# Another order at the entry of the tree-expert stage, node-logit bias on ScalarE, five sums of x on GpSimd

## The chip, the cores and the metric

The kernel runs on one core of one Trainium2 chip. The metric is the device time of one execution in microseconds (us), and less is better. The core's engines are TensorE (PE, with its weight loads as PEld), VectorE (DVE), ScalarE (ACT), GpSimd (POOL) and SyncE (SP). Each has a queue of its own and works it off in order; they wait for each other by semaphores only.

## The reference, cut to what matters

The program is a stack of four layers on 1250 tokens of width 512: a graph network with batch norm, routed experts, a second graph aggregation, and a tree of experts. Only the last one is touched by the change. In short:

```python
def _leaf_probs(flat_x, rw, rb):                 # 7 nodes, 8 leaves
    for d in range(3):
        logits = flat_x @ rw[off:off+n].T + rb[off:off+n]
        p = sigmoid(logits)
        leaf = (leaf[:, :, None] * stack([1 - p, p], 2)).reshape(n_tok, 2 * n)
x  = x + aggregate(layernorm(x)) @ weight.T      # the layer before, "produce" in the kernel
f  = layernorm(x)
h  = gelu(einsum('nd,edh->neh', f, w1) + b1)     # 8 experts, 512 -> 2048
y  = einsum('neh,ehd->ned', h, w2) + b2          # 2048 -> 512
x  = x + einsum('ned,ne->nd', y, leaf)
```

## The kernel before, in words

The tree stage is `phase_tree` (from L1603). Its work is cut by hidden columns: 64 groups G of 256 columns, eight for each expert. For each G, TensorE computes the first layer and for each pair of groups (a quarter Q) the second. Every float32 product is split into a high and a low part, and `cut_products` (L526 to L530) makes three matmuls of it.

The first layer is a fast matrix product. The tokens lie in three blocks of 418, 418 and 414 and x (transposed, `f_xT`) in four slices of 128. From these VectorE makes 20 sums, the forms (`x_forms`, by `total` L2222 and `less_both` L2226), with eight helper sums (`x_parts`). ScalarE rounds the forms in ten pairs to a high part (`form_highs`, L1830) and VectorE takes the low part (`form_lows`, L2231). Each pair is 836 columns wide. The forms are needed in the order of `FORM_ORDER`: pair 0 is forms 6 and 11, then 18 and 15, and so on. 15 sums of the weights are made for each G by GpSimd (`weight_sums`, L1772), rounded by ScalarE (`w_high`, L1838), and VectorE takes the rest in three instructions (`w_rest`, L2104): two on raw weights, one on the 14 sums, 1792 columns wide. `first_layer(G)` on TensorE waits at its start for all three of its G (`w_lo >= 3 * (G + 1)`).

TensorE then multiplies 20 forms in an order written by hand. Product names follow the PSUM bank that they close: D B1 C1 A1 (forms 6, 11, 18, 15), A2 (5), E (10), B2 (9), A3 (13, 16), B3 (0, 4), A4 (7), F (14), B4 (17), A5 (1, 19), B5 (2, 8), C2 (3), A6 (12). Between products VectorE adds banks into `hidden` in the order T12 T00 O00 T02 O02 T01 T11 V O12 O01 O11 (the `mix_` functions), and ScalarE copies banks out (P6, V, P18, F2, F6, A4). Product A2 waits for T12, B3 for F6, A4 for T00, B5 for T01.

Before that comes the entry of the stage. For each of the ten token tiles TensorE runs `produce` (the layer before), VectorE adds it to `x_rows` and takes the statistics, ScalarE writes normalized rows, TensorE turns them (`turn`, L1972), and ScalarE copies them into `f_xT` (`moved`, L1864). `logits(b)` (L1982) multiplies the node weights with token block b, `node_logits(b)` (L2219) adds the bias from `rb_col`, and `node_turn(b)` (L1989) turns the result. ScalarE makes the branch probabilities from it (L1922), and GpSimd the leaf weights (L1818, L1822).

All orders are written out by hand, one list for each engine, in one block with no scheduler. On SP the next raw weights are loaded once VectorE is through with the old: `load2(1)` waits for `w2_rest(0)`, and `load1(2)`, behind it, for the two raw parts of `w_rest(1)` and the sums of GpSimd.

Of the kernel before, what the change touches and what calls it, by code (L numbers as in the profile page):

```python
# [1602 lines left out]
def phase_tree(nc, sem, g, produce, rows):  # L1603
# [49 lines left out]

    FORM_ORDER = (6, 11, 18, 15, 5, 10, 9, 13, 16, 0, 4, 7, 14, 17, 1, 19, 2, 8, 3, 12)
    FORM_AT = {form: i for i, form in enumerate(FORM_ORDER)}
    SUMS = counts("A B F8 E F16 F F1 F5 H I F6 C F11 F7 F18 G F15 F10 F3 F14 F9 F13 F17 F4 F19 F2 F12")
    PART_AT = {name: 2 + i for i, name in enumerate("HICGEFAB")}

    U1, U2, U3, U4, U5, U6, U7, U8, U9, U10, U11, U12, U13, U15, H0K0, H1K0, H0K2, H0K3 = range(WFORMS)
# [75 lines left out]
    with nc.Block() as block:  # L1735
        @block.sync
        def _(sp):
            def load1(n):
                e, p = divmod(n, 8)
                if n:  # L1740
                    sp.wait_ge(w_lo, 3 * (n - 1) + 2)
                    sp.wait_ge(w_sum, w_summed(n - 1, "U13"))
                sp.dma_start(raw1[:, :, :], w1_d[e, :, :, p * 256:(p + 1) * 256]).then_inc(w1_in, 16)

            def load2(n):
                e, p = divmod(n, 8)
                if n:
                    sp.wait_ge(w2_lo, n)
                sp.dma_start(raw2[:, :, :], w2_d[e, :, 2 * p:2 * p + 2, :]).then_inc(w2_in, 16)

            load1(0)
            load2(0)
            load1(1)
            for G in range(GROUPS):
                if G % 8 == 0:
                    e = G // 8
                    if e == 0:
                        sp.wait_ge(node_turned, 1)
# [12 lines left out]

        @block.gpsimd  # L1772
        def _(q):
# [53 lines left out]

        @block.scalar
        def _(a):
            def form_highs(p, *after):  # L1830

                for name in after:
                    a.wait_ge(x_sum, SUMS[name])
                a.activation(form_high(2 * p, 2 * p + 2), g.xsum[:, 2 * p:2 * p + 2, :], ACT.Copy).then_inc(x_hi, 1)  # L1834

            def w_high(n):
# [10 lines left out]
            def w2_high(n):  # L1847
                a.wait_ge(w2_in, 16 * (n + 1))
                if n == 0:
                    a.wait_ge(x_sum, len(SUMS))  # L1850
                    a.wait_ge(noded, 3)
                if n >= 2:
                    a.wait_ge(used, y_count(n // 2 - 1, NT - 1))
                a.activation(w2hi[:, n % 2], raw2[:, :, :], ACT.Copy).then_inc(w2_hi, 1)

            for i in range(NT + 3):
                j = i - 2
                if 0 <= j < NT:
# [12 lines left out]
                if i == 7:
                    a.wait_ge(moved, 4)
                    a.activation(form_sum(0), x_block(2, 2), ACT.Copy, scale=-1.0).then_inc(x_unit, 1)
            a.wait_ge(produced, NT)
            form_highs(0, "F6", "F11")
            form_highs(1, "F18", "F15")
            form_highs(2, "F5", "F10")
            form_highs(3, "F9", "F13")
            a.wait_ge(x_unit, 1)
            form_highs(4, "F16")  # L1880
            form_highs(5, "F4", "F7")
            form_highs(6, "F6", "F14", "F17")
            form_highs(7, "F11", "F15", "F1", "F19")
            form_highs(8, "F16", "F19", "F2", "F8")
            form_highs(9, "F17", "F3", "F12")

            def bias(G, j):
                at = G // 8 * 16 + G % 8 * 2 + j
# [77 lines left out]
        def _(t):  # L1966
# [115 lines left out]
            t.wait_ge(added, 8)  # L2082
            logits(1)
            turn(8)
            t.wait_ge(added, NT)
            node_turn(0)
            turn(9)
            logits(2)
            node_turn(1)
            node_turn(2).then_inc(node_turned, 1)  # L2090
            t.wait_ge(moved, NT)
            for G in range(GROUPS):
# [9 lines left out]

        @block.vector
        def _(v):  # L2104
            def w_rest(n):
                to, of = g.wlo[n % 2], g.whi[n % 2]
                v.wait_ge(w_hi, 3 * n + 1)
                v.tensor_tensor(to[:, H0K0:H1K0 + 1, :].rearrange("p u c -> p (u c)"), raw1[:, 0, :],
                                of[:, H0K0:H1K0 + 1, :].rearrange("p u c -> p (u c)").bitcast(F32),
                                ALU.subtract).then_inc(w_lo, 1)  # L2110
                v.wait_ge(w_hi, 3 * n + 2)
                v.tensor_tensor(to[:, H0K2:H0K3 + 1, :], raw1[:, 2:4, 0:128], of[:, H0K2:H0K3 + 1, :].bitcast(F32),
                                ALU.subtract).then_inc(w_lo, 1)
                v.wait_ge(w_hi, 3 * n + 3)
                v.tensor_tensor(to[:, U1:U15 + 1, :], g.wsum[n % 2][:, U1:U15 + 1, :],  # L2115
                                of[:, U1:U15 + 1, :].bitcast(F32), ALU.subtract).then_inc(w_lo, 1)

            def w2_rest(n):
                v.wait_ge(w2_hi, n + 1)
# [96 lines left out]
            def node_logits(b):
                lo, hi = TBLOCKS[b]
                v.wait_ge(noded, b + 1)
                v.tensor_scalar(g.node_z[:, lo:hi], g.psum[0:7, LOGIT_BANK[b], 0:hi - lo], g.rb_col[0:7, :], None,  # L2219
                                ALU.add).then_inc(biased, 1)  # L2220

            def total(to, a, op, b):  # L2222

                v.tensor_tensor(to, a, b, op).then_inc(x_sum, 1)  # L2224
# [3 lines left out]
                v.scalar_tensor_tensor(out=to, in0=a, scalar=-1.0, in1=b, op0=ALU.mult,  # L2228
                                       op1=ALU.subtract).then_inc(x_sum, 1)

            def form_lows(p, last_reader=None):  # L2231
                v.wait_ge(x_hi, p + 1)
                if last_reader:
                    v.wait_ge(x_sum, SUMS[last_reader])
# [26 lines left out]
            node_logits(0)  # L2261
# [14 lines left out]
            node_logits(1)  # L2276
# [7 lines left out]
            node_logits(2)  # L2284
# [8 lines left out]
            v.wait_ge(x_sum, SUMS["F3"])  # L2293
            total(form_sum(17), part("A"), ALU.subtract, form_sum(3))
            total(form_sum(4), x_block(3, 2), ALU.subtract, form_sum(9))
            total(form_sum(19), form_sum(1), ALU.subtract, part("F"))
            total(form_sum(2), x_block(3, 1), ALU.add, form_sum(3))
            total(form_sum(12), form_sum(7), ALU.subtract, x_block(3, 0))
# [236 lines left out]
```

## Time and profile before

| | us |
|---|---|
| median of 3 runs | 2312.99 |
| lowest, highest | 2309.54, 2313.89 |
| the profiled execution | 2310.99 |
| its span, from the first to the last instruction | 2309.0 |
| PE busy | 2171.3 (94%) |
| PEld busy | 1906.3 (83%) |
| DVE busy | 1606.3 (70%) |
| ACT busy | 1059.3 (46%) |
| POOL busy | 634.5 (27%) |
| mean granted PE clock | 0.976 |

A busy share is a mean over the whole span. Times inside the program are counted from the span's start. The tree stage's entry lies at about 608 to 685 us, and the 64 groups follow until the end. A clock of 1.00 is 2.4 GHz and one of 0.50 is 1.2 GHz.

### The profile page before, as it was taken

The numbers are of one execution on the slowest core, as the hardware profiler recorded it, in microseconds if no ns is written. First come the engines' busy times: TensorE is split into PE (matmuls) and PEld (weight loads), VectorE is DVE, ScalarE is ACT, GpSimd is POOL, SyncE is SP. The second block draws the span as 40 slices with busy tenths as digits, with TensorE's granted clock in tenths as the row PEclk, the third lists the DMA queues.
The fourth block names the chain that finished last, engine by engine and source line by source line (L and its number), as shares of the span: only waits on it lengthen the run. The fifth ranks groups of instructions, "written<-read, shape, count | busy, mean of one in ns | idle before, by whom it ended". The sixth has DMA issues, their size and how long they took to land.

```text
span 2309.0 us, 32827 instructions
## 1 busy us (share of the span) xinstructions
PE 2171.3 (94%) x11871; PEld 1906.3 (83%) x11871; DVE 1606.3 (70%) x2619; ACT 1059.3 (46%) x1862; POOL 634.5 (27%) x1081
## 2 busy tenths in 40 slices
PE   3997998597979999999999999999999999999998
PEld 3887996467858888888888888888888888888887
DVE  7996355736487776777777667777776777777665
ACT  0335334344354544545554444554544455554443
POOL 0554000011133233223322322243233223323320
PEclk9999999598989999999999999999999999999999
DMA  2000201151001111111111111111111111111111
GB/s 71 3 2 1 73 1 64 65 173 45 28 23 37 46 51 37 37 49 48 37 38 59 38 37 37 60 37 37 46 51 37 38 58 39 37 39 58 37 37 54
DMA packets 70701, 102.00 MB, mean 44 GB/s; under 512 B 5519, under 2 KB 40927, under 8 KB 70543
## 3 DMA queue, kind: packets, MB, share of 16 engines
q1 hardware_dynamic: 67243, 94.20, 12.8%
q0 software_dynamic: 3040, 5.19, 0.7%
q8 instruction: 97, 1.59, 0.3%
q14 instruction: 61, 0.50, 0.1%
q10 hardware_dynamic: 260, 0.51, 0.1%
HBM read 92.14 MB, written 7.74 MB: 43 GB/s over the span
## 4 chain that ended last, share of the span: by engine, by line
PE 72%; DVE 1%; ACT 1%; issue 0%; DVEq 0%; ACTq 0%
PE psum L528 24%; PE psum L529 24%; PE psum L530 24%; DVE x_forms L2224 0%; DVE x_parts L2224 0%; ACT w_forms_hi L1845 0%; PE psum L1972 0%; DVE x_forms_lo L2235 0%; ACT x_forms_hi_late L1834 0%; DVE node_z L2219 0%; ACT f_rows L522 0%; DVE x_rows L2244 0%; DVE stats L486 0%; ACT L1922 0%; DVE x_forms L2228 0%
## 5 line engine op out<-in xcount | busy, mean ns | idle before, releaser
L530 PE MATMUL psum<-w_hi,hidden_lo 128*125 128x512 f32 x1280 | 505.2, 395 | 0.0
L529 PE MATMUL psum<-w_lo,hidden_hi 128*125 128x512 f32 x1280 | 504.8, 394 | 0.0
L528 PE MATMUL psum<-w_hi,hidden_hi 128*125 128x512 f32 x1280 | 504.6, 394 | 0.0
L529 PE MATMUL psum<-x_forms_lo,w_forms_hi 128*128 128x418 f32 x1280 | 453.6, 354 | 0.0
L1782 POOL TENSOR_TENSOR w_forms<-w_raw 128x128 f32<-128x128 f32 x192 | 107.0, 585 | 1159.1 <-PE psum L530 597.7
L2212 DVE SCALAR_TENSOR_TENSOR x_rows<-psum,leaf_by_token,x_rows 125x512 f32<-125x512 f32 x320 | 233.8, 747 | 258.3 <-PE psum L530 258.3
L1895 ACT ACTIVATE hidden<-psum 128x418 f32<-128x418 f32 (+1 forms) x320 | 164.5, 514 | 487.9 <-PE psum L530 485.3
L530 PEld LDWEIGHTS psum<-w_hi,hidden_lo 128*125 128x125 f32 x1280 | 237.1, 185 | 60.0
L528 PEld LDWEIGHTS psum<-w_hi,hidden_hi 128*125 128x125 f32 x1280 | 237.1, 185 | 56.6 <-issue 0.5
L529 PEld LDWEIGHTS psum<-w_lo,hidden_hi 128*125 128x125 f32 x1280 | 237.3, 185 | 55.1
L2185 DVE TENSOR_TENSOR hidden_lo<-hidden,hidden_hi 128x418 fp32r<-128x418 f32 (+1 forms) x384 | 256.5, 693 | 21.8 <-ACT hidden_hi L1917 21.8
L1907 ACT ACTIVATE hidden<-hidden,b1cols 128x418 f32<-128x418 f32 (+1 forms) x320 | 204.5, 639 | 105.1 <-DVE hidden L2140 95.2
L529 PEld LDWEIGHTS psum<-x_forms_lo,w_forms_hi 128*128 128x128 f32 x1280 | 243.0, 190 | 8.7
L528 PE MATMUL psum<-x_forms_hi_first,w_forms_hi 128*128 128x418 f32 x640 | 228.4, 357 | 7.2 <-DVE hidden L2129 5.1
L528 PE MATMUL psum<-x_forms_hi_late,w_forms_hi 128*128 128x418 f32 x640 | 227.9, 356 | 0.0
L530 PE MATMUL psum<-x_forms_hi_first,w_forms_lo 128*128 128x418 f32 x640 | 227.7, 356 | 0.0
L1782 POOL TENSOR_TENSOR w_forms<-w_raw,w_forms 128x128 f32<-128x128 f32 x384 | 225.2, 594 | 5.0
L530 PE MATMUL psum<-x_forms_hi_late,w_forms_lo 128*128 128x418 f32 x640 | 225.5, 352 | 0.0
L1917 ACT ACTIVATE hidden_hi<-hidden 128x418 fp32r<-128x418 f32 (+1 forms) x384 | 204.5, 550 | 6.1
L2115 DVE TENSOR_TENSOR w_forms_lo<-w_forms,w_forms_hi 128x1792 fp32r<-128x1792 f32 x64 | 129.6, 2026 | 37.4 <-ACT w_forms_hi L1845 37.4
L1782 POOL TENSOR_TENSOR w_forms<-w_forms,w_raw 128x128 f32<-128x128 f32 x256 | 137.9, 539 | 5.0
L528 PEld LDWEIGHTS psum<-x_forms_hi_first,w_forms_hi 128*128 128x128 f32 x640 | 121.8, 190 | 15.8 <-DVE hidden L2129 5.4
(346 smaller groups left out, 3511.5 us busy)
## 6 DMA issues: line engine op xcount, KB each, us to landing
w_raw<-in_w SPq DMA_DIRECT2D x128, 512.0 KB, 3.9
expert_raw<-in_experts SPq DMA_DIRECT2D x8, 1024.0 KB, 5.6
expert_results_d<-expert_results SPq DMA_DIRECT2D x16, 160.0 KB, 4.8
x_rows<-in_x SPq DMA_DIRECT2D x1, 2500.0 KB
c_rows_d<-c_rows SPq DMA_DIRECT2D x10, 250.0 KB
W_raw<-in_gnn_W SPq DMA_DIRECT2D x4, 512.0 KB, 4.1
W_raw<-in_gnn_W SPq DMA_DIRECT2D x1, 2048.0 KB, 9.5
b_by_token<-in_b SPq DMA_DIRECT2D x8, 256.0 KB, 3.9
```

The lines of the kernel that those rows point to most:

```text
L528: t.matmul(out, stat[0], mov[0], start=start, stop=False, skip_group_check=again)
L529: t.matmul(out, stat[0], mov[1], start=False, stop=False, skip_group_check=again)
L530: return t.matmul(out, stat[1], mov[0], start=False, stop=stop, skip_group_check=again)
L1782: q.tensor_tensor(u[:, to, :], a, b, op).then_inc(w_sum, 1)
L1895: a.activation(slot_of(hid, G, b, j), g.psum[:, bank, 0:width(b)], ACT.Copy, scale=scale).then_inc(copied, 1)
L1907: a.activation(to, to, ACT.Gelu, bias=bias(G, j)).then_inc(active, 1)
L1917: a.activation(slot_of(hhi, G, b, j), slot_of(hid, G, b, j), ACT.Copy).then_inc(hi_cut, 1)
L2115: v.tensor_tensor(to[:, U1:U15 + 1, :], g.wsum[n % 2][:, U1:U15 + 1, :], of[:, U1:U15 + 1, :].bitcast(F32), ALU.subtract).then_inc(w_lo, 1)
L2185: v.tensor_tensor(slot_of(hlo, G, b, j), slot_of(hid, G, b, j), slot_of(hhi, G, b, j).bitcast(F32), ALU.subtract).then_inc(lo_cut, 1)
L2212: v.scalar_tensor_tensor(out=g.x_rows[:, i, :], in0=g.psum[0:TR, i % Y_BANKS, :], scalar=g.leaf[:, i, e:e + 1], in1=g.x_rows[:, i, :], op0 ...
```

## The change

It has four parts, all in `phase_tree`.

1. On TensorE `turn(9)` comes right behind `turn(8)`, and `node_turn(1)` ahead of `logits(2)`.
2. The three `node_logits` go from VectorE, where they lay between the sums of x, to ScalarE, ahead of `form_highs(0)`.
3. Five of the 27 sums of x (forms 4, 12, 17, 19 and 2) go from VectorE to GpSimd, with a semaphore of their own, `f_x_sum_pool`.
4. On VectorE, the low parts 7, 8 and 9 of x, which came ahead of everything of group 0, are put between the mixes of group 0. `w_rest(1)` is cut in two: its raw parts come ahead of T00, and the part on the sums comes behind O11, with `w2_rest(0)` and the `low` calls of group 0 behind it.

```diff
     SUMS = counts("A B F8 E F16 F F1 F5 H I F6 C F11 F7 F18 G F15 F10 F3 F14 F9 F13")
+    POOL_SUMS = counts("F4 F12 F17 F19 F2")
 # gpsimd, behind weight_sums(1)
+            q.wait_ge(x_sum, SUMS["F7"])
+            q.wait_ge(moved, NT)
+            q.wait_ge(x_sum, SUMS["F9"])
+            form_total(form_sum(4), x_block(3, 2), ALU.subtract, form_sum(9))
+            form_total(form_sum(12), form_sum(7), ALU.subtract, x_block(3, 0))
+            form_total(form_sum(17), part("A"), ALU.subtract, form_sum(3))
+            form_total(form_sum(19), form_sum(1), ALU.subtract, part("F"))
+            form_total(form_sum(2), x_block(3, 1), ALU.add, form_sum(3))
 # scalar
+            def node_logits(b):
+                lo, hi = TBLOCKS[b]
+                a.wait_ge(noded, b + 1)
+                a.activation(g.node_z[:, lo:hi], g.psum[0:7, LOGIT_BANK[b], 0:hi - lo], ACT.Identity,
+                             bias=g.rb_col[0:7, :]).then_inc(biased, 1)
             a.wait_ge(produced, NT)
+            for b in range(3):
+                node_logits(b)
             form_highs(0, "F6", "F11")
...
-            form_highs(5, "F4", "F7")
-            form_highs(6, "F6", "F14", "F17")
-            form_highs(7, "F11", "F15", "F1", "F19")
-            form_highs(8, "F16", "F19", "F2", "F8")
-            form_highs(9, "F17", "F3", "F12")
+            form_highs(5, "F7", pool="F4")
+            form_highs(6, "F6", "F14", pool="F17")
+            form_highs(7, "F11", "F15", "F1", pool="F19")
+            form_highs(8, "F16", "F8", pool="F2")
+            form_highs(9, "F18", "F3", pool="F2")
 # tensor
             turn(8)
+            turn(9)
             t.wait_ge(added, NT)
             node_turn(0)
-            turn(9)
+            node_turn(1)
             logits(2)
-            node_turn(1)
             node_turn(2).then_inc(node_turned, 1)
 # vector: node_logits(0), (1), (2) and the five sums go, and
-            form_lows(3, "F4")
+            form_lows(3, pool="F4")
             form_lows(4, "F13")
-            form_lows(5, "F12")
+            form_lows(5, pool="F12")
             mix_t12(0)
             form_lows(6)
-            form_lows(7, "F19")
+            w_rest_raw(1)
+            mix_t00(0)
+            mix_o00(0)
+            mix_t02(0)
+            form_lows(7, pool="F19")
+            mix_o02(0)
+            mix_t01(0)
             form_lows(8)
-            form_lows(9, "F2")
-
-            for G in range(GROUPS):
+            mix_t11(0)
+            form_lows(9, pool="F2")
+            mix_v(0)
+            mix_o12(0)
+            mix_o01(0)
+            mix_o11(0)
+            w_rest_sums(1)
+            w2_rest(0)
+            low(0, 2, 0)
+            low(0, 0, 0)
+            low(0, 0, 1)
+
+            for G in range(1, GROUPS):
```

TensorE at the end of the entry, before. L1972 is `turn`, L1982 `logits` and L1989 `node_turn`:

```order
L1972 MATMUL psum<-small_consts,f_rows 128x125 x4
L1982 MATMUL psum<-f_xT,vecs 7x418 x4
L1972 MATMUL psum<-small_consts,f_rows 128x125 x4
L1989 MATMUL psum<-small_consts,node_z 125x7 x3
L1972 MATMUL psum<-small_consts,f_rows 128x125 x4
L1982 MATMUL psum<-f_xT,vecs 7x414 x4
L1989 MATMUL psum<-small_consts,node_z 125x7 x7
```

The same place of the changed kernel, where L1999 is `turn`, L2009 `logits` and L2016 `node_turn`:

```order
L1999 MATMUL psum<-small_consts,f_rows 128x125 x4
L2009 MATMUL psum<-f_xT,vecs 7x418 x4
L1999 MATMUL psum<-small_consts,f_rows 128x125 x8
L2016 MATMUL psum<-small_consts,node_z 125x7 x6
L2009 MATMUL psum<-f_xT,vecs 7x414 x4
L2016 MATMUL psum<-small_consts,node_z 125x7 x4
```

The last two tiles are turned in one go, and two of the three node turns stand ahead of the last logits.

VectorE in group 0, before. L2235 is `form_lows`, L2108 to L2115 `w_rest(1)`, L2120 `w2_rest(0)`; the last row is T00, behind which the other mixes follow:

```order
L2129 TENSOR_TENSOR hidden<-psum,hidden 128x418
L2235 TENSOR_TENSOR x_forms_lo<-x_forms,x_forms_hi_late 128x836 x4
L2108 TENSOR_TENSOR w_forms_lo_10989<-w_raw,w_forms_hi_10988 128x256
L2112 TENSOR_TENSOR w_forms_lo_10989<-w_raw,w_forms_hi_10988 128x256
L2115 TENSOR_TENSOR w_forms_lo_10989<-w_forms_10990,w_forms_hi_10988 128x1792
L2120 TENSOR_TENSOR w_lo<-w_raw,w_hi 128x1024
L2135 TENSOR_TENSOR hidden<-psum,hidden 128x414
```

The changed kernel from T02 (first row) on. L2265 is `form_lows`, L2201 V, L2215 O11 and L2145 the part of `w_rest(1)` on the sums:

```order
L2180 TENSOR_TENSOR hidden<-psum,hidden 128x418
L2265 TENSOR_TENSOR x_forms_lo<-x_forms,x_forms_hi_late 128x836
L2186 TENSOR_TENSOR hidden<-psum,hidden 128x418
L2192 TENSOR_TENSOR hidden<-hidden,psum 128x418
L2265 TENSOR_TENSOR x_forms_lo<-x_forms,x_forms_hi_late 128x836
L2197 TENSOR_TENSOR hidden<-hidden,psum 128x418
L2265 TENSOR_TENSOR x_forms_lo<-x_forms,x_forms_hi_late 128x836
L2201 TENSOR_TENSOR v_part<-v_part,psum 128x418
L2206 TENSOR_TENSOR hidden<-hidden,v_part 128x418
L2211 TENSOR_TENSOR hidden<-psum,hidden 128x418
L2215 TENSOR_TENSOR hidden<-hidden,v_part 128x418
L2145 TENSOR_TENSOR w_forms_lo_10989<-w_forms_10990,w_forms_hi_10988 128x1792
```

Three low parts of x now stand between the mixes, and the 1792 columns of weight sums of group 1 stand behind O11, where they stood ahead of T00.

## Rows read from the trace of the kernel before

**Rows 1.** Stretches: us, busy us (count) per engine, then PEclk, DMA share, GB/s.
```profile
649.50:652.00 2.50, 1.03 (x7) 0.81 (x7) 0.76 (x2) 1.01 (x2) 0.97 (x2) 0.99 0.00 0
652.00:655.00 3.00, 2.89 (x5) 0.64 (x6) 2.77 (x5) 0.06 (x1) 0.00 (x0) 0.50 0.00 0
655.50:658.50 3.00, 1.63 (x7) 0.52 (x5) 2.93 (x6) 0.90 (x1) 0.00 (x0) 1.00 0.00 0
...
675.80:679.00 3.20, 3.12 (x9) 2.98 (x10) 3.20 (x3) 2.66 (x4) 0.00 (x0) 0.50 0.00 0
...
700.00:2300.00 1600.00, 1600.00 (x7537) 1402.38 (x7536) 1153.84 (x1705) 780.76 (x1372) 491.24 (x915) 1.00 0.14 43
```
**Rows 2.** Waits of PE, 640 to 720 us: total us, times, longest.
```profile
PE psum L528 <- DVE hidden L2129: 5.1, 1, 5.1
```
**Rows 3.** Timeline of PE: start us, us, what, idle before and its releaser.
```profile
648.71 0.65 PE L1972 MATMUL psum<-small_consts,f_rows 125*128 125x125 f32 x4
...
679.78 0.39 PE L528 MATMUL psum<-x_forms_hi_late,w_forms_hi 128*128 128x418 f32 x1
...
682.73 0.35 PE L528 MATMUL psum<-x_forms_hi_late,w_forms_hi 128*128 128x418 f32 x1
...
683.89 0.35 PE L528 MATMUL psum<-x_forms_hi_late,w_forms_hi 128*128 128x418 f32 x1
...
685.03 0.35 PE L528 MATMUL psum<-x_forms_hi_first,w_forms_hi 128*128 128x418 f32 x1
```
**Rows 4.** Timeline of DVE, same columns.
```profile
652.10 0.60 DVE L2228 SCALAR_TENSOR_TENSOR x_forms<-f_xT 128x418 f32<-128x418 f32 x1 [1.84 <-ACT f_xT L1864]
...
661.32 1.03 DVE L2235 TENSOR_TENSOR x_forms_lo<-x_forms,x_forms_hi_first 128x836 fp32r<-128x836 f32 x1
662.27 1.09 DVE L2224 TENSOR_TENSOR x_forms<-f_xT,x_forms 128x418 f32<-128x418 f32 x2
...
670.84 0.59 DVE L2129 TENSOR_TENSOR hidden<-psum,hidden 128x418 f32<-128x418 f32 x1 [0.27 <-ACT hidden L1895]
671.35 3.91 DVE L2235 TENSOR_TENSOR x_forms_lo<-x_forms,x_forms_hi_late 128x836 fp32r<-128x836 f32 x4
...
676.01 2.01 DVE L2115 TENSOR_TENSOR w_forms_lo<-w_forms,w_forms_hi 128x1792 fp32r<-128x1792 f32 x1
...
684.09 0.59 DVE L2167 TENSOR_TENSOR v_part<-v_part,psum 128x418 f32<-128x418 f32 x1 [0.56 <-PE psum L530]
```
**Rows 5.** Timeline of ACT, same columns.
```profile
649.40 0.59 ACT L1864 ACTIVATE f_xT<-psum 128x500 f32<-128x500 f32 x1 [2.20 <-PE psum L1972]
651.47 0.59 ACT L1864 ACTIVATE f_xT<-psum 128x500 f32<-128x500 f32 x1 [1.49 <-PE psum L1972]
...
666.28 4.06 ACT L1834 ACTIVATE x_forms_hi_late<-x_forms 128x836 fp32r<-128x836 f32 x5 [1.14 <-DVE x_forms L2224]
670.25 0.49 ACT L1895 ACTIVATE hidden<-psum 128x418 f32<-128x418 f32 x1
```
**Rows 6.** Groups by shape (busy us, mean ns): ACT on a PSUM tile of few partitions.
```profile
L1247 ACT ACTIVATE gates_T<-psum 8x418 f32<-8x418 f32 x1 | 0.5, 492 | 0.0
```
**Rows 7.** GpSimd sums by line: duration ns min/median/max.
```profile
L466 POOL TENSOR_TENSOR weight_sum<-weight_parts x40: 857/870/1262, 49.6 to 194.1; 128x320 f32<-128x320 f32 x40
...
L632 POOL TENSOR_TENSOR x_rows<-x_rows,xn x10: 1269/1290/1304, 199.2 to 216.5; 125x512 f32<-125x512 f32 x10
```
**Rows 8.** Timelines of POOL and DVE where both read SBUF.
```profile
199.24 1.27 POOL L632 TENSOR_TENSOR x_rows<-x_rows,xn 125x512 f32<-125x512 f32 x1 [3.29 <-ACT xn L522]
...
199.85 1.20 DVE L829 TENSOR_TENSOR xn_hi_lo<-xn,xn_hi_lo 125x512 fp32r<-125x512 f32 x1 [1.54 <-ACT xn_hi_lo L689]
...
647.33 0.84 DVE L2224 TENSOR_TENSOR x_parts<-x_parts,f_xT 128x418 f32<-128x418 f32 x1
...
647.68 0.80 POOL L1782 TENSOR_TENSOR w_forms<-w_forms,w_raw 128x128 f32<-128x128 f32 x1
```
**Rows 9.** DMA issues, 660 to 730 us: count, KB each, median us to landing.
```profile
w_raw<-in_w SPq DMA_DIRECT2D x4, 512.0 KB, 3.7
```

More of the change, by code:

```diff
@@ L1618, in phase_tree @@
     x_sum = sem("f_x_sum")
+    x_sum_pool = sem("f_x_sum_pool")
     x_hi = sem("f_x_hi")
@@ L1655, in phase_tree @@
     FORM_AT = {form: i for i, form in enumerate(FORM_ORDER)}
-    SUMS = counts("A B F8 E F16 F F1 F5 H I F6 C F11 F7 F18 G F15 F10 F3 F14 F9 F13 F17 F4 F19 F2 F12")
+    SUMS = counts("A B F8 E F16 F F1 F5 H I F6 C F11 F7 F18 G F15 F10 F3 F14 F9 F13")
+    POOL_SUMS = counts("F4 F12 F17 F19 F2")
     PART_AT = {name: 2 + i for i, name in enumerate("HICGEFAB")}
@@ L1759, in _ @@
                         sp.wait_ge(x_sum, len(SUMS))
+                        sp.wait_ge(x_sum_pool, len(POOL_SUMS))
                         sp.wait_ge(x_unit, 1)
@@ L1815, in _, with form_total @@
             weight_sums(1)
+            def form_total(to, a, op, b):
+                q.tensor_tensor(to, a, b, op).then_inc(x_sum_pool, 1)
+            q.wait_ge(x_sum, SUMS["F7"])
[6 more added lines that the diff above has]
+            form_total(form_sum(2), x_block(3, 1), ALU.add, form_sum(3))
             q.wait_ge(branched, 2)
@@ L1829, in _, with form_highs @@
         def _(a):
-            def form_highs(p, *after):
+            def form_highs(p, *after, pool=None):
                 for name in after:
                     a.wait_ge(x_sum, SUMS[name])
+                if pool:
+                    a.wait_ge(x_sum_pool, POOL_SUMS[pool])
                 a.activation(form_high(2 * p, 2 * p + 2), g.xsum[:, 2 * p:2 * p + 2, :], ACT.Copy).then_inc(x_hi, 1)
@@ L1850, in w2_high @@
                     a.wait_ge(x_sum, len(SUMS))
+                    a.wait_ge(x_sum_pool, len(POOL_SUMS))
                     a.wait_ge(noded, 3)
@@ L2104, in _, with w_rest_raw @@
         def _(v):
-            def w_rest(n):
+            def w_rest_raw(n):
                 to, of = g.wlo[n % 2], g.whi[n % 2]
@@ L2113, in w_rest, with w_rest_sums @@
                                 ALU.subtract).then_inc(w_lo, 1)
+            def w_rest_sums(n):
+                to, of = g.wlo[n % 2], g.whi[n % 2]
                 v.wait_ge(w_hi, 3 * n + 3)
@@ L2116, in w_rest @@
                                 of[:, U1:U15 + 1, :].bitcast(F32), ALU.subtract).then_inc(w_lo, 1)
+            def w_rest(n):
+                w_rest_raw(n)
+                w_rest_sums(n)
             def w2_rest(n):
@@ L2214, in add_y @@
                                        op0=ALU.mult, op1=ALU.add).then_inc(y_added, 1)
[L2216 to L2220, printed above, removed]
             def total(to, a, op, b):
@@ L2229, in less_both, with form_lows @@
                                        op1=ALU.subtract).then_inc(x_sum, 1)
-            def form_lows(p, last_reader=None):
+            def form_lows(p, after=None, pool=None):
                 v.wait_ge(x_hi, p + 1)
-                if last_reader:
-                    v.wait_ge(x_sum, SUMS[last_reader])
+                if after:
+                    v.wait_ge(x_sum, SUMS[after])
+                if pool:
+                    v.wait_ge(x_sum_pool, POOL_SUMS[pool])
                 v.tensor_tensor(g.xlo[:, 2 * p:2 * p + 2, :], g.xsum[:, 2 * p:2 * p + 2, :],
@@ L2260, in _ @@
             total(part("F"), part("B"), ALU.subtract, x_block(2, 1))
-            node_logits(0)
             v.wait_ge(moved, NT)
@@ L2275, in _ @@
             total(form_sum(11), part("B"), ALU.add, part("C"))
-            node_logits(1)
             total(form_sum(7), part("F"), ALU.subtract, x_block(2, 0))
@@ L2283, in _ @@
             total(form_sum(10), x_block(0, 0), ALU.subtract, form_sum(11))
-            node_logits(2)
             total(form_sum(3), x_block(0, 1), ALU.add, form_sum(11))
@@ L2292, in _ @@
             form_lows(2, "F9")
[L2293 to L2298, printed above, removed]
-            form_lows(3, "F4")
+            form_lows(3, pool="F4")
             form_lows(4, "F13")
-            form_lows(5, "F12")
+            form_lows(5, pool="F12")
             mix_t12(0)
             form_lows(6)
-            form_lows(7, "F19")
-            form_lows(8)
-            form_lows(9, "F2")
-            for G in range(GROUPS):
+            w_rest_raw(1)
[5 more added lines that the diff above has]
+            mix_t01(0)
+            form_lows(8)
+            mix_t11(0)
[10 more added lines that the diff above has]
+            for G in range(1, GROUPS):
                 Q = G // 2
-                if G:
-                    mix_t12(G)
+                mix_t12(G)
                 if G % 2:
@@ L2318, in _ @@
                     w_rest(G + 1)
-                    if Q:
-                        add_y(Q - 1, LATE)
-                        add_y(Q - 1, LATE + 1)
+                    add_y(Q - 1, LATE)
+                    add_y(Q - 1, LATE + 1)
                     w2_rest(G)
```

## The prediction

> **What bounds the kernel now.** First the table of stretches. From 700 to 2300 us TensorE is busy all 1600 of 1600 us at clock 1.00 [rows 1], so nothing that other engines save there moves the end. The change touches only what lies before, where TensorE does wait, and the time of the kernel follows the moment at which TensorE starts group 1, 685.03 now [rows 3]. Then the waits of TensorE: the longest, 5.1 us, is for T12 on VectorE [rows 2], which itself waits for ScalarE's copy P6 at 670.25 [rows 4, 5]. That copy stands behind `form_highs(9)`, the last of five in a row from 666.28 [rows 5], which began when VectorE had made form 4. Last the timelines, to see what each engine does around these points. From T12 on there is one order on three engines, and it is there that VectorE's list is rewritten.
>
> **Entry up to the first low part.** VectorE stands 1.84 us until the last tile is in `f_xT` and takes it up at 652.10 [rows 4]. With `turn(9)` right behind `turn(8)` (648.71, 0.65 us) it ends at about 649.9; ScalarE, which copied tile 8 at 649.40, copies tile 9 at 649.95 where it was 651.47 [rows 3, 5]. VectorE starts at 650.6, 1.5 us earlier. Two of the three bias instructions lay behind this point; a step of 418 columns takes a slot of 0.50 us (1.09 for two, less 0.59) [rows 4]. So the first low part starts 1.5 + 2 x 0.55 = 2.6 us earlier, at 658.7 instead of 661.32. ScalarE must have its first high part by then. The bias costs it 0.5 us each [rows 6], bounds 0.4 and 0.6 from its PSUM copies [rows 5], and the third waits for `logits(2)`, which now starts behind two node turns at about 651.8 and ends by 656.3; bias 2 ends at 656.9 and the high part at 657.8. It is hidden, with 0.9 us to spare. Forms 9 and 13, the slots behind the first low part, end at 660.2 and 660.7 (662.27 before).
>
> **Five sums on GpSimd.** At 128x418 it has no row. Alone, its 320 columns take 0.86 us and 512 take 1.29 [rows 7], which gives 1.07 for 418. But the inputs of these sums, and of the low parts that VectorE takes meanwhile, are all in SBUF, and there the two engines exclude each other: at 199.85 VectorE, started inside GpSimd's 1.27 us, takes 1.20 us and ends 0.54 behind GpSimd's end, that is its own stream after the other's; at 647 us both go up, to 0.84 and 0.80 [rows 8]. I take alternation. GpSimd then holds the port about 0.95 us (1.07 less its start), a low part of 836 columns 0.87 of its 0.96 slot (3.91 for four) [rows 4], together 1.83. Form 4 gets the port at 660.6; form 4, 12, 17, 19 and 2 end at 661.6, 663.4, 665.2, 667.0 and 668.8, and low part 5 at 669.7. `form_highs(8)` needs form 2: 668.8; (9) is 0.8 behind it ((4.06 - 0.88) / 4 [rows 5]), the copy P6 another 0.8, at 670.4, and T12 at 671.0. Before it was 670.84. So 2.6 us of earlier start and five slots taken from VectorE come to +0.2 us: what is late next is form 2. Bounds: with a free port form 2 ends at 660.2 + 5 x 1.07 = 665.6 and T12 starts 2.2 behind it as above, at 667.8, -3.0; if GpSimd loses one more turn of 0.9, T12 is at 671.9, +1.0. Since T12 stands behind low part 5, port work alone (660.6 + 5 x 0.95 + 5 x 0.87) puts it at 669.7 or later.
>
> The Trainium skill (Perfetto Trace Analysis, Optimizing Scalar/DVE Operations) warns that moving elementwise work from VectorE to GpSimd might not help, since they share an SBUF read port. The trace agrees, 1.20 us for VectorE's instruction; by a free port the total below would be 3.2 us less.
>
> **ScalarE behind T12** keeps its list (P6, V, P18, table, branches, `w_high(1)`, F2), so product A3 comes +0.2 later and TensorE's forms 0 and 4 end near 679.98 (679.78 [rows 3]). VectorE now does low part 6 and the raw parts of `w_rest(1)`, waits for them until about 674, and then has nothing until A3 at 678.5. This idle time held the 2.01 us on the weight sums before [rows 4].
>
> **Three low parts between the mixes.** T02 waits for B3, 680.2. Then slots: T02 0.5, low 7 1.0, O02 0.5, T01 0.5, low 8 1.0 give 683.7. TensorE wants form 2 (low 8) at 682.73 + 0.2 [rows 3]: +0.9 wait, where there was none. T11 0.5 and low 9 end at 685.2, form 3 is wanted at 683.89 + 0.2 + 0.9 = 685.0: +0.3. V starts at 685.2, +1.1 against 684.09 [rows 4]. Bounds of these two waits: 0 (if all slots shrink) and 2.0.
>
> **The weight sums behind O11.** `first_layer(1)` waits for them. V, O12, O01 and O11 take four slots, 2.15 us, and the sums 2.01 [rows 4]: 685.2 + 4.16 = 689.4. Before, TensorE started group 1 at 685.03, 0.94 behind V. Now it cannot start earlier than 4.2 behind V, whatever comes ahead, since V itself waits for B5 and TensorE has only forms 3 and 12 left. So +3.3 from this edit alone. Sum up to group 1: 0.2 + 0.9 + 3.3 = **+4.4 us**, TensorE at 689.45 with a pause of about 2.8 us.
>
> Queued behind the moved instructions: `w2_rest(0)` ends at 690.5 and three `low` calls at 692.1. TensorE needs them behind four forms of group 1, from 691.8, in turn: no wait. SP issues `load2(1)` and `load1(2)` at 690.5 and after, instead of 679; they land 3.7 us later [rows 9], 694.2 to 695.5. ScalarE wants W2 at about 697, GpSimd starts its sums for group 2 ten us late and ends by 705, ahead of ScalarE's need at about 708. Cover is 2 to 3 us; without it the excess would be lost. Later groups are as before.
>
> **The clock.** Group 1 starts behind pauses of 0.9, 0.3 and 2.8 us. In the stretch from 649.5 to 652 TensorE was busy 1.03 of 2.50 us and the clock then stood at 0.50 until about 655.4, and at 1.00 from 655.5 [rows 1]. I take one such stretch of 3.4 us. At 0.50 nine matmuls of 418 columns fill 3.12 us, 0.35 each, at 1.00 three take 0.57 ((685.03 - 683.89) / 2, two forms [rows 3]), 0.19 each; half the work is lost: +1.6 us. Bounds 0 and +3.4 (twice as long). The sum is **+6.0 us**.
>
> The Trainium skill (TensorE: Matmul & The Clock Gate, HAM oscillation) counts only idle gaps longer than any pause I expect here. By that rule the clock stays and the sum is +4.4. The trace disagrees: it fell with TensorE busy 41% of the stretch [rows 1].
>
> **The time.** The profiled execution took 2310.99 us with a span of 2309.0; the median of the runs shown is 2312.99. I set out from the middle of the two, 2312.0, and get 2318.0 (span 2315.0 in the terms of the profile).
>
> **Rivals.**
> - *Port contended, clock stays* (the rule of the page above): +4.4, 2316.4. For it: from 655.5 to 658.5 TensorE was busy 1.63 of 3.00 us, and the clock was at 1.00 throughout [rows 1]. Against it: the fall at 652.
> - *Port free*: GpSimd does not hold up VectorE, T12 at 667.8, -3.0 + 4.2 + 1.6 = +2.8, 2314.8. For it: VectorE's low parts may leave gaps. Against it: both rows of contention.
> - *Not slower*: the port is free and, with the pause before T12 a us shorter, the clock is at 1.00 for the four forms 13, 16, 0 and 4, which stood at 0.50 in 675.8 to 679 [rows 1]. They save 4 x 0.47 = 1.9 us, and the clock doesn't fall later: -3.0 - 1.9 + 4.2 = -0.7, 2311.3. It decides if form 2 ends before 666 and TensorE is at full clock at A3. The clock now stands at 0.50 there behind the pause of 5.1.
> - *Long low stretch*: TensorE stays at 0.50 twice as long at group 1, or GpSimd loses turns: +8, 2320.
> - *Something here pays more than I see* (the change doesn't do at O11 what I read): faster than 2307.4.
>
> **Chances.** Forecast 50%, clock stays 15%, port free 13%, not slower 8%, long low stretch 9%, more 5%. The range from 2310.8 to 2322.5 leaves out the last and tails of the others. A measurement of this kernel tells 0.2%, 4.6 us, from no change. Slower by more: 42 of the 50 of the forecast, 5 of 15, 1 of 13, 9 of 9: 0.57. Faster: the last 5 and 2 of the not-slower: 0.07. Within: 0.36.
>
> **What would show it.** VectorE's first sum behind `f_xT` at about 650.6 and its first low part at 658.7; the five sums on GpSimd 1.07 us each if alone and up to 2 if not, and low parts 1 to 5 stretched to 1.8; T12 at 671 within 1; VectorE idle ahead of T00; TensorE waiting for low parts 8 and 9, about 1.2 together, then 2.5 to 3 us for `w_rest_sums(1)`; the clock at 0.50 behind it for some 3 us; no wait on DMA in groups 1 and 2; 1.00 and no pause from 700. Wrong would be: group 1 started by anything but `w_lo`, or started within 2 us behind V, or T12 earlier than 669.

## The result and the profile after

| | before | changed |
|---|---|---|
| median of 10 runs, us | 2311.94 | 2316.53 |
| lowest, highest | 2309.2, 2313.89 | 2313.7, 2318.6 |
| span of the profiled execution | 2309.0 | 2311.5 |

The changed kernel takes 1.0022 of the time before, 95% interval 1.0013 to 1.0030: it is slower by 0.0022 x 2312 = 5.1 us (3.0 to 6.9); the two medians differ by 4.6. Forecast were +6.0 us.

The part ahead of the change has the same instructions in all kernels here, yet its end lay up to 3.8 us apart in their profiles (sum A at 644.58 to 648.42 us), so places in the entry are counted below from the start of helper sum A on VectorE (645.06 us before, 644.58 changed), the first work that the change can reach. "V3" is the V mix of group 3. From it to the last add to `x_rows` the two kernels differ by 0.2 us.

| us from sum A | before | changed |
|---|---|---|
| first sum behind `f_xT` | 7.04 | 5.43 |
| first low part | 16.26 | 13.56 |
| T12 | 25.78 | 25.81 |
| V of group 0 | 39.03 | 38.68 |
| TensorE starts group 1 | 39.97 | 42.90 |
| V3 | 104.48 | 108.81 |

Waits of PE in the changed kernel, 640 to 725 us (total us, times, longest), in answer to [rows 2]:

```profile
PE psum L528 <- DVE hidden L2163: 6.7, 1, 6.7
PE psum L528 <- DVE w_forms_lo L2145: 2.8, 1, 2.8
PE psum L528 <- DVE x_forms_lo L2265: 2.7, 3, 2.0
PE psum L2016 <- ACT node_z L1896: 2.0, 2, 1.3
```

The wait for T12 is 6.7 us where it was 5.1: TensorE is earlier at it, T12 is not. The second line is new, the wait for the weight sums behind O11. Of the third, 0.56 us is the wait for low part 8 (below); the 2.0 lies in the first forms, ahead of T12.

VectorE in the changed kernel (start, us, what, idle before), in answer to [rows 4]:

```profile
650.01 0.59 DVE L2256 SCALAR_TENSOR_TENSOR x_forms<-f_xT 128x418 f32<-128x418 f32 x1 [0.79 <-ACT f_xT L1882]
...
658.14 1.03 DVE L2265 TENSOR_TENSOR x_forms_lo<-x_forms,x_forms_hi_first 128x836 fp32r<-128x836 f32 x1
659.09 1.09 DVE L2252 TENSOR_TENSOR x_forms<-f_xT,x_forms 128x418 f32<-128x418 f32 x2
660.09 7.06 DVE L2265 TENSOR_TENSOR x_forms_lo<-x_forms,x_forms_hi_first 128x836 fp32r<-128x836 f32 x4
667.08 1.89 DVE L2265 TENSOR_TENSOR x_forms_lo<-x_forms,x_forms_hi_late 128x836 fp32r<-128x836 f32 x1
670.39 0.59 DVE L2163 TENSOR_TENSOR hidden<-psum,hidden 128x418 f32<-128x418 f32 x1 [1.42 <-ACT hidden L1922]
...
676.88 0.59 DVE L2169 TENSOR_TENSOR hidden<-psum,hidden 128x414 f32<-128x414 f32 x1 [2.83 <-PE psum L530]
...
683.26 0.59 DVE L2201 TENSOR_TENSOR v_part<-v_part,psum 128x418 f32<-128x418 f32 x1
...
685.40 2.02 DVE L2145 TENSOR_TENSOR w_forms_lo<-w_forms,w_forms_hi 128x1792 fp32r<-128x1792 f32 x1
```

Four low parts take 7.06 us, where four of the same size (6 to 9, behind T12) took 3.91 [rows 4], and VectorE stands 2.83 us ahead of T00, where `w_rest(1)` used to be. GpSimd's five sums, in the order of forms 4, 12, 17, 19, 2:

```profile
659.85 1.11 POOL L1821 TENSOR_TENSOR x_forms<-f_xT,x_forms 128x418 f32<-128x418 f32 x1 [9.78 <-DVE x_forms L2252]
660.92 1.87 POOL L1821 TENSOR_TENSOR x_forms<-x_forms,f_xT 128x418 f32<-128x418 f32 x1
662.75 1.85 POOL L1821 TENSOR_TENSOR x_forms<-x_parts,x_forms 128x418 f32<-128x418 f32 x1
664.56 1.71 POOL L1821 TENSOR_TENSOR x_forms<-x_forms,x_parts 128x418 f32<-128x418 f32 x1
666.23 1.85 POOL L1821 TENSOR_TENSOR x_forms<-f_xT,x_forms 128x418 f32<-128x418 f32 x1
```

The first one starts at 659.85, ahead of low part 1, which then has to wait for it, and takes 1.11 us; the others alternate with the low parts.

ScalarE, in answer to [rows 5, 6]: tile 9 follows tile 8 at once, two biases take 1.07 us together, and copy P6 stands behind the last two high parts, which waited for GpSimd:

```profile
648.91 1.07 ACT L1882 ACTIVATE f_xT<-psum 128x500 f32<-128x500 f32 x2 [2.19 <-PE psum L1999]
649.86 1.07 ACT L1896 ACTIVATE node_z<-psum,rb_col 7x418 f32<-7x418 f32 x2
...
668.20 1.69 ACT L1851 ACTIVATE x_forms_hi_late<-x_forms 128x836 fp32r<-128x836 f32 x2 [0.91 <-POOL x_forms L1821]
669.79 0.50 ACT L1922 ACTIVATE hidden<-psum 128x418 f32<-128x418 f32 x1
```

TensorE, in answer to [rows 3]: the last product ahead of form 2, the wait for low part 8, the first product of form 3, and the wait ahead of group 1:

```profile
680.95 0.35 PE L530 MATMUL psum<-x_forms_hi_late,w_forms_lo 128*128 128x418 f32 x1
681.86 0.43 PE L528 MATMUL psum<-x_forms_hi_late,w_forms_hi 128*128 128x418 f32 x1 [0.56 <-DVE x_forms_lo L2265]
...
682.88 0.35 PE L530 MATMUL psum<-x_forms_hi_late,w_forms_lo 128*128 128x418 f32 x1
683.30 0.43 PE L528 MATMUL psum<-x_forms_hi_late,w_forms_hi 128*128 128x418 f32 x1
...
687.48 0.46 PE L528 MATMUL psum<-x_forms_hi_first,w_forms_hi 128*128 128x418 f32 x1 [2.80 <-DVE w_forms_lo L2145]
```

Products start 0.19 us apart where nothing holds them. Form 2 starts 0.91 behind the product before it and form 3 0.42, so they are 0.7 and 0.2 us late. Behind 687.48 TensorE has no pause: the later loads of weights hold up nothing, as predicted.

Stretches of the changed kernel, columns as in [rows 1], the third from the right being the clock:

```profile
672.00:675.00 3.00, 2.54 (x8) 1.90 (x6) 0.93 (x2) 2.99 (x7) 0.83 (x2) 0.50 0.00 0
675.00:679.00 4.00, 3.57 (x17) 3.23 (x18) 1.94 (x4) 3.84 (x6) 0.00 (x0) 0.97 0.00 0
685.00:688.00 3.00, 0.53 (x3) 0.52 (x4) 3.00 (x3) 1.94 (x4) 0.00 (x0) 1.00 0.00 0
689.00:692.00 3.00, 3.00 (x10) 2.61 (x9) 2.14 (x5) 2.37 (x5) 0.00 (x0) 0.50 0.73 217
693.00:700.00 7.00, 7.00 (x37) 6.64 (x37) 4.22 (x8) 3.91 (x7) 5.93 (x13) 1.00 0.03 10
700.00:2300.00 1600.00, 1600.00 (x7541) 1403.20 (x7540) 1156.71 (x1710) 782.33 (x1375) 492.31 (x918) 1.00 0.13 43
```

The clock was back at 1.00 from about 675.2, ahead of form 13; in the kernel before it stood at 0.50 until about 679.2 [rows 1]. Behind the pause ahead of group 1 it fell to 0.50, at about 688.9, and from about 692.3 it was up again. From 700 on TensorE has no pause in either kernel. Of the 4.33 us at V3 the spans show only 2.5: this execution began 0.48 earlier, V3 to the last add to `x_rows` took 0.2 less, and the stores behind that 1.2 less.

### The profile page after: what moved, and what is told of

It is laid out like the page before. It is cut to its first block, busy times and chain, and to the rows that moved or that the text cites. A ratio compares the mean times of both kernels' runs of the same rounds, so it can differ in the third digit from the quotient of the medians.

```text
span 2311.5 us, 32830 instructions
## 1 busy us (share of the span) xinstructions
PE 2172.1 (94%) x11871; PEld 1906.0 (82%) x11871; DVE 1604.2 (69%) x2611; ACT 1061.3 (46%) x1865; POOL 638.5 (28%) x1086
## 4 chain that ended last, share of the span: by engine, by line
PE 72%; DVE 1%; ACT 0%; POOL 0%; issue 0%; POOLq 0%; DVEq 0%; ACTq 0%
PE psum L528 24%; PE psum L529 24%; PE psum L530 24%; POOL x_forms L1821 0%; PE psum L2009 0%; DVE x_forms L2252 0%; PE psum L1999 0%; ACT w_forms_hi L1862 0%; DVE x_parts L2252 0%; DVE x_forms_lo L2265 0%; DVE w_forms_lo L2145 0%; ACT hidden L1922 0%; ACT L1949 0%; DVE x_forms L2256 0%; ACT f_xT L1882 0%
## 5 line engine op out<-in xcount | busy, mean ns | idle before, releaser
L2145 DVE TENSOR_TENSOR w_forms_lo<-w_forms,w_forms_hi 128x1792 fp32r<-128x1792 f32 x64 | 129.6, 2026 | 37.4 <-ACT w_forms_hi L1862 37.4
```

## The experiments

Ratios are to the kernel before, in the same batch of runs.

| run | T12 | V of group 0 | group 1 | V3 | ratio (95%) |
|---|---|---|---|---|---|
| before | 25.8 | 39.0 | 40.0 | 104.5 | 1 |
| changed | 25.8 | 38.7 | 42.9 | 108.8 | 1.0022 (1.0013 to 1.0030) |
| sums of w early | 25.8 | 40.4 | 41.3 | 107.0 | 1.0008 (0.9998 to 1.0017) |
| parts 1, 2, 3 | 25.8 | 39.7 | 40.6 | 105.1 | 1.0003 (0.9994 to 1.0012) |
| parts 1, 2, 4 | 23.2 | 37.6 | 41.8 | 107.7 | 1.0011 (1.0001 to 1.0020) |
| parts 1, 2 | 23.1 | 36.6 | 37.6 | 102.1 | 0.9987 (0.9978 to 0.9996) |
| low parts together | 25.8 | 37.7 | 41.9 | 108.9 | 1.0016 (1.0007 to 1.0026) |
| part 4 alone | 25.8 | 40.4 | 44.6 | 110.6 | 1.0021 (1.0012 to 1.0030) |
| PSUM operand | 22.7 | 37.2 | 41.4 | 107.4 | one execution, no ratio |
| pause filled | 25.8 | 40.5 | 44.7 | 109.1 | 1.0013 (1.0004 to 1.0022) |
| parts 1, 2, W2 late, fill | 23.2 | 37.0 | no wait | 102.0 | 0.9985 (0.9976 to 0.9994) |
| parts 1, 2, W2 late | 23.2 | 35.8 | no wait | 100.8 | 0.9989 (0.9980 to 0.9998) |

**Weight sums back ahead of T00.**

```diff
-            w_rest_raw(1)
+            w_rest(1)
...
             mix_o11(0)
-            w_rest_sums(1)
```

> The changed kernel, with the weight-sum part of w_rest(1) back ahead of T00; all else stays. Times are counted from the start of helper sum A on VectorE; the changed kernel has T12 at 25.8, V of group 0 at 38.7, TensorE's group 1 at 42.9 and V of group 3 at 108.8, the kernel before 25.8, 39.0, 40.0 and 104.5. Theory: the 2.8 us pause ahead of group 1 comes from this one placement, and the clock falls behind it. Then T12 and V stay within 0.5, group 1 starts at 40 to 40.5 with no wait on w_lo, no stretch at 0.50 follows, V of group 3 is at 104.5 to 105, and the time is 4 us below the changed kernel, ratio to the kernel before 1.000 to 1.001. Rival (VectorE's total work is the limit, the order doesn't matter): T12 to V grows by the 2 us of the sums, group 1 comes less than 1 us earlier, ratio 1.002.

The wait on `w_lo` is gone, and once up, the clock stays at 1.00; V to V3 takes 66.6 us against 70.1. But three places miss their ranges: V of group 0 is at 40.4, where it was to stay within 0.5 of 38.7, group 1 at 41.3 and V3 at 107.0. The waits for low parts 8 and 9 stay, the clock rose late (35 us from sum A), and there is a new wait of TensorE, since `w2_rest(0)` and the `low` calls still lie behind O11:

```profile
PE psum L528 <- DVE hidden_lo L2219: 0.8, 1, 0.8
```

The ratio is at the upper end of the theory's range. The interval (0.9998 to 1.0017) overlaps that of the changed kernel, so the traces have to tell the size: against part 4 alone (below), whose clock rose as late and which has the same V of group 0, group 1 starts 3.3 us earlier (41.3 against 44.6). The placement of the sums is most of the loss, not all.

**Parts 1, 2 and 3** (VectorE's list of group 0 as before).

```diff
             form_lows(6)
-            w_rest_raw(1)
+            form_lows(7, pool="F19")
+            form_lows(8)
+            form_lows(9, pool="F2")
+            w_rest(1)
+            w2_rest(0)
             mix_t00(0)
...
```

> Parts 1, 2 and 3 of the change, with VectorE's list of group 0 as in the kernel before. Theory: GpSimd's sums give back all of the earlier start, so T12 is at 25.6 to 26.1, group 1 at 39.5 to 40.5, V of group 3 at 104 to 105, ratio 1.000. Rival (the sums on GpSimd are a gain that the new order of group 0 hides): T12 at 23 to 24.5 and ratio 0.999.

T12 at 25.83: GpSimd's sums give back the whole earlier start. Ratio 1.0003. As in the theory, with group 1 at 40.6 and V3 at 105.1, each 0.1 above its range.

**Parts 1, 2 and 4** (the five sums on VectorE, where they were).

> Parts 1, 2 and 4, with the five sums of x back on VectorE. Theory: without GpSimd in the way the 2.6 us of parts 1 and 2 reach T12, at 23.1 to 23.5; the pause of about 2.8 us ahead of group 1 stays, with the stretch at 0.50 behind it; group 1 at 40 to 41, V of group 3 at 105.5 to 106.5, ratio 1.0005 to 1.0015. Rival (the sums on GpSimd relieve VectorE): T12 at 28, five slots of 0.5 us behind the changed kernel's, ratio 1.003 or more.

T12 at 23.16 with the same list of mixes. The pause ahead of group 1 is 2.83 us again. Group 1 at 41.8 and V3 at 107.7 lie 0.8 and 1.2 above their ranges, as the base of my figures, the changed kernel's profile, had a lucky clock (below). The rival is out: VectorE does five more sums and is at T12 2.65 us earlier.

**Parts 1 and 2 alone** (against the kernel before).

```diff
             turn(8)
+            turn(9)
...
+            for b in range(3):
+                node_logits(b)
             form_highs(0, "F6", "F11")
```

> Parts 1 and 2 alone: TensorE's order and the bias on ScalarE, on the kernel before. Theory: T12 at 23.1 to 23.5, group 1 at 37.3 to 38 and V of group 3 at 101.5 to 102.5, 2.6 us less than before, ratio 0.9985 to 0.9995, the best of all. Rival (the bias on ScalarE or the copies behind it become the limit): T12 at 25 or later, ratio 1.000.

T12 at 23.14, V3 2.4 us ahead of the kernel before, ratio 0.9987 (0.9978 to 0.9996). All as in the theory. VectorE's T12 in this kernel still waits for ScalarE's copy, only earlier on this scale (sum A is at 647.80 here):

```profile
669.59 1.02 DVE L2250 TENSOR_TENSOR x_forms_lo<-x_forms,x_forms_hi_late 128x836 fp32r<-128x836 f32 x1
670.94 0.59 DVE L2148 TENSOR_TENSOR hidden<-psum,hidden 128x418 f32<-128x418 f32 x1 [0.33 <-ACT hidden L1907]
```

**Low parts 7 to 9 together.**

```diff
             form_lows(6)
+            form_lows(7, pool="F19")
+            form_lows(8)
+            form_lows(9, pool="F2")
             w_rest_raw(1)
...
             mix_o00(0)
             mix_t02(0)
-            form_lows(7, pool="F19")
...
```

> The changed kernel with low parts 7, 8 and 9 of x together again behind low part 6; the weight sums stay behind O11. Times from the start of helper sum A. Theory: only the waits for low parts 8 and 9 go (0.56 us and a gap of 0.3); the pause ahead of group 1 stays 2.8 us. T12 25.8, group 1 at 41.8 to 42.4 (42.9 changed), V of group 3 at 107.5 to 108.3 with a stretch at 0.50 behind the pause, ratio 1.0015 to 1.002. Rival (the interleaving was what cost most, as the low parts stand in the way of the mixes): group 1 at 41 or earlier, ratio 1.001 or less.

Group 1 at 41.89, the one us less that the theory has, but the pause grew to 3.11 us and V3 did not gain. The clock fell inside the pause this time, and stood at 0.50 from about 687.4 to 694.2, twice as long as in the changed kernel:

```profile
688.00:694.00 6.00, 5.61 (x15) 5.12 (x16) 4.00 (x7) 2.97 (x6) 0.00 (x0) 0.50 0.52 170
```

This is the "long low stretch" of the prediction, seen once. The ratio of 1.0016 agrees with the theory; its V3 does not.

**Part 4 alone, on the kernel before.**

> Part 4 of the change alone, on the kernel before: VectorE's new order of group 0, no more. Theory: T12 as before, 25.8, group 1 about 2.7 us behind that of parts 1, 2 and 4 (41.8), at 44 to 45, V of group 3 at 109.5 to 111, ratio 1.002 to 1.0025, the whole loss of the change. Rival (the loss needs the earlier start or the sums on GpSimd as well): ratio 1.001 or less.

Ratio 1.0021, the whole loss, with T12, group 1 and V3 in their ranges. V3 is at +6.1 us; this profile is of a long execution, 2318.88 us where the median of this kernel is 2316.54. Here are the terms of the prediction in one trace, sum A being at 648.22:

```profile
688.60 0.59 DVE L2174 TENSOR_TENSOR v_part<-v_part,psum 128x418 f32<-128x418 f32 x1
...
690.74 2.02 DVE L2118 TENSOR_TENSOR w_forms_lo<-w_forms,w_forms_hi 128x1792 fp32r<-128x1792 f32 x1
```
```profile
692.82 0.46 PE L528 MATMUL psum<-x_forms_hi_first,w_forms_hi 128*128 128x418 f32 x1 [2.81 <-DVE w_forms_lo L2118]
```

Group 1 starts 4.2 us behind V, where it was 0.94.

**A second operand in PSUM** (the low parts 1 to 5 don't compete for the port).

```diff
+                other = g.psum[:, 2:4, 0:TBW] if 1 <= p <= 5 else form_high(2 * p, 2 * p + 2).bitcast(F32)
...
                 v.tensor_tensor(g.xlo[:, 2 * p:2 * p + 2, :], g.xsum[:, 2 * p:2 * p + 2, :],
-                                form_high(2 * p, 2 * p + 2).bitcast(F32), ALU.subtract).then_inc(x_lo, 1)
+                                other, ALU.subtract).then_inc(x_lo, 1)
```

> The changed kernel with low parts 1 to 5 reading their second operand from two PSUM banks instead of from the high part in SBUF, which leaves out the true low parts of ten forms. It takes GpSimd's rival away from the port. Theory: the five sums on GpSimd take 1.07 to 1.11 us each instead of 1.85, the low parts 1.0 us instead of 1.8, and T12 comes at 22.5 to 23.3 instead of 25.8. Rival (GpSimd is slow at this width by itself, or by waits between its sums): the sums stay at 1.7 or more and T12 at 25 or later.

The last four of GpSimd's sums, then VectorE's low parts, of this kernel:

```profile
664.14 1.08 POOL L1821 TENSOR_TENSOR x_forms<-x_forms,f_xT 128x418 f32<-128x418 f32 x1
665.18 1.08 POOL L1821 TENSOR_TENSOR x_forms<-x_parts,x_forms 128x418 f32<-128x418 f32 x1
666.22 0.92 POOL L1821 TENSOR_TENSOR x_forms<-x_forms,x_parts 128x418 f32<-128x418 f32 x1
667.11 1.07 POOL L1821 TENSOR_TENSOR x_forms<-f_xT,x_forms 128x418 f32<-128x418 f32 x1
```
```profile
663.31 4.76 DVE L2266 TENSOR_TENSOR x_forms_lo<-x_forms,psum 128x836 fp32r<-128x836 f32 x5
```

1.08 us against 1.85, and 0.95 a low part against 1.8. Both engines work on the same number of elements; only where one operand lies has changed. T12 comes at 22.70, 3.1 us earlier. So what holds the sums is VectorE's second read of SBUF, which is what the prediction called the port.

**The pause filled.**

```diff
+                if G == 1:
+                    for _ in range(12):
+                        t.matmul(g.psum[:, 0, 0:TBW], g.whi[0][:, U1, :], form_high(0, 1)[:, 0, :],
+                                 start=True, stop=True)
                 first_layer(G)
```

> The changed kernel with 12 extra matmuls of 418 columns into an idle PSUM bank, in TensorE's pause ahead of group 1 (2.3 us of 2.8 at full clock). Theory: the stretch at 0.50 behind the pause comes from the pause and costs 1.6 us. Then group 1 starts at 42.9 as in the changed kernel, the clock stays at 1.00 through groups 0 and 1, V of group 3 is at 107.1 to 107.5 instead of 108.8, ratio 1.0013 to 1.002. Rival (the fall has its cause further ahead, in the pause before T12 or in the grid of the clock): the stretch at 0.50 comes all the same, V of group 3 at 108.5 or later.

The clock stayed at 1.00 around and behind the pause:

```profile
688.00:691.00 3.00, 2.60 (x14) 2.23 (x12) 3.00 (x5) 2.23 (x4) 0.00 (x0) 1.00 0.00 0
691.00:694.00 3.00, 2.87 (x14) 2.74 (x15) 2.98 (x6) 1.88 (x4) 0.00 (x0) 1.00 0.18 47
```

V to V3 takes 68.6 us against 70.1: the low stretch cost 1.5 us and came from the pause. In the kernel with part 4 alone the clock also rose late (35.1), and fell to 0.50 behind the unfilled pause, so the late rise is not what kept the clock up here. V3 itself was at 109.1, not 107.1 to 107.5: by its number that is the rival's, but the rival's cause, a fall all the same, did not happen. V was at 40.5 where the changed kernel's profile has 38.7, with the same instructions up to there. The difference is the moment at which the clock rose, 35.7 us from sum A here and 30.7 there. The ratio of 1.0013 is as expected, though its interval overlaps that of the changed kernel.

**Toward a better version.** To parts 1 and 2, `w2_rest(0)` moved behind T11, once with extra matmuls in TensorE's two pauses and once without.

```diff
             w_rest(1)
-            w2_rest(0)
             mix_t00(0)
...
             mix_t11(0)
+            w2_rest(0)
             mix_v(0)
```

> Parts 1 and 2, with w2_rest(0) moved from ahead of T00 to behind T11, and with 10 and 14 extra matmuls of 384 columns into an idle PSUM bank in TensorE's pauses ahead of the first form and ahead of T12. Theory: T12 stays at 23.1 (it waits for ScalarE); the extra matmuls keep the clock at 1.00 through the entry, so forms 13 to 4 take 0.57 us each; T00 comes at 30.2 to 30.6 instead of 31.4; V of group 3 at 100.3 to 101.2 instead of 102.1, ratio 0.998 to 0.9985. Rival (VectorE's list sets T00 whatever the clock, and the clock's low stretch is hidden): V of group 3 at 101.8 or later.

The filling failed. The extra matmuls took only part of the wait for T12, and 3.35 us of it stayed; its waits, then two stretches:

```profile
PE psum L528 <- DVE hidden L2157: 3.4, 1, 3.4
PE psum L528 <- ACT hidden L1907: 2.0, 1, 2.0
```
```profile
670.00:671.00 1.00, 1.00 (x5) 0.73 (x4) 1.00 (x2) 0.99 (x5) 0.22 (x1) 0.69 0.00 0
671.00:674.00 3.00, 0.97 (x3) 0.64 (x3) 3.00 (x5) 3.00 (x4) 1.87 (x2) 0.50 0.00 0
```

The longer wait ended at 668.96 and the second one ran until 673.35. The clock fell between them, within 670 to 671, where TensorE was busy without a gap, and was low in the first forms behind the second. V3 is at 102.0, so the theory's number is missed and the rival's (101.8 or later) is met. What would happen at full clock stays open, since the clock did not stay up.

> Parts 1 and 2, with w2_rest(0) behind T11 and no extra matmuls. Theory: T00 can come 0.8 to 1.1 us earlier, but as long as the clock is at 0.50 until 33 or so TensorE itself is not there before: V of group 3 at 101.5 to 102.1 against 102.1 of parts 1 and 2, ratio 0.9985 to 0.999. Rival (T00 on VectorE holds TensorE at either clock): V of group 3 at 101.1 or earlier.

V3 is at 100.8, in the rival's range; but here the clock had risen by 673.4, 27.3 us from sum A, where parts 1 and 2 alone have 32.3, so one profile doesn't decide between them. In time the three versions with parts 1 and 2 (0.9987, 0.9985, 0.9989) can't be told apart. Each is faster than the kernel before and the changed one; parts 1 and 2 alone are the simplest.

## Why the prediction was right

- **Entry, 2.6 us:** the first low part came 2.70 us earlier (16.26 to 13.56), 1.61 of it from `turn(9)`. The bias on ScalarE was hidden, at 0.5 us each.
- **Five sums on GpSimd, +0.2:** measured +0.03 at T12. Alternation at 1.83 us was the right model: the sums took 1.71 to 1.87. Returning them to VectorE, or moving VectorE's second operand to PSUM, gave 2.65 and 3.1 us. The rivals with a free port fall. The warning of the Trainium skill (Perfetto Trace Analysis, Optimizing Scalar/DVE Operations) held: moving the sums did not help.
- **Waits for low parts 8 and 9, +0.9 and +0.3:** the two forms came 0.7 and 0.2 us late, 0.9 together against 1.2. With the low parts together again, and the clock rising at the same moment, V and group 1 came 1.0 us earlier. (The +0.9 is 0.1 more than its own slots give, 683.7 less 682.93.) T12 to V took 14.4 to 14.7 us in the interleaved kernels with a late clock, and 13.2 to 13.9 in those with the list as before.
- **Weight sums behind O11, +3.3:** 4.2 us from V to group 1 in the changed kernel, the one with part 4 alone, and that with parts 1, 2 and 4, against 0.94: 3.3 more in each.
- **The clock, +1.6:** it fell behind the pause in all of these, and the filled pause gave 1.5 us back. The rival in which the clock stays falls: behind pauses of 0.56 and 2.80 us with work between them it fell. By the rule of the Trainium skill (TensorE: Matmul & The Clock Gate, HAM oscillation) pauses this short would have left it alone; the traces disagree.
- **The sum, +6.0:** measured 5.1 (3.0 to 6.9) by the ratio, 4.6 by the medians. The trace of part 4 alone has +6.1 at V3, its terms being +1.4 up to V of group 0, +3.3 to group 1 and +1.4 behind it; as it is of a long execution, the close match with 6.0 is in part luck.
- **Group 1, +4.4:** missed by the one profile of the changed kernel (+2.9), for a cause that the prediction had only as a part of a rival, *not slower*: the clock rose 3.5 us earlier than before, counted from sum A, and forms 13 to 4 ran at 1.00. The rival priced that at 1.9 us; V of group 0 lay at 38.7 instead of 40.5 with the same code up to there, in the kernel with the filled pause, which had 44.7 for group 1, +4.7.

That the early rise is chance from one execution to the next is concluded, not shown, but more than these two traces speak for it. The clock rose 8.4 to 9.9 us behind T12 in nine of the twelve profiles of this case, and 4.1 to 4.8 us behind it in three: the changed kernel, the low parts together, and parts 1 and 2 with W2 late. And the changed kernel's profile is of the fastest of its ten executions, 2313.70 us where the median is 2316.53. What sets the moment stays open.

Part by part: parts 1 and 2 gain 2.4 us at V3 (3.0 by the ratio), part 3 gives all of it back (T12 at 25.8 again, ratio 1.0003), and part 4 alone costs 4.9 (1.0021). `turn(9)` and the bias were not run apart.

## What to carry to other kernels

Before work is moved from VectorE to GpSimd, see whether what VectorE does meanwhile reads two operands from SBUF: then both may take turns, as here, where a low part of VectorE took 1.8 us instead of 0.95 and a sum of GpSimd 1.85 instead of 1.08. Before an instruction is moved behind others on its engine, look up who waits for its semaphore and count from the last thing ahead of it: here 2 us of work left a place where VectorE had time for it and landed between the last mix and the next group's first product. Compare entries by distances between two marks in the same trace, and note at which clock each stretch ran, before a difference is put down to the code.

## What the runs showed of the hardware

- A GpSimd sum of two SBUF operands, 128x418 float32, takes 1.71 to 1.87 us while VectorE runs instructions that read two SBUF operands of 836 columns. Where VectorE has one of the two in PSUM, the sum takes 0.92 to 1.11 us and the low part 1.02, as it does with GpSimd idle.
- Short pauses can bring the clock down: it fell to 0.50 behind pauses of 0.56 and 2.80 us with 2.4 us of work between them. In the kernel with the weight sums early it stayed at 1.00 through pauses of 0.56 and 0.81.
- The clock can fall while TensorE is at work: in the version of parts 1 and 2 with extra matmuls it fell between 670 and 671, a microsecond that matmuls fill without a gap, 1 to 2 us after a wait of 3.35 us had ended.
- With the same code up to there, the clock rose at 30.7 us from sum A in one trace and at 35.7 in another, and V of group 0 moved by 1.8 us with it, where the whole effect looked for is 4.6 to 5.1 us.
